# Attention and gated feed-forward on one core: group 0's first keys and queries through identity products, its row maxima on both sides of the array, the turns of heads later

## What is computed

```python
xn = layernorm(x)                                   # x: 1024 tokens x 512, f32
q, k, v = xn@wq+bq, xn@wk+bk, xn@wv+bv              # 32 heads of q, 8 of k and v, 16 values each
q, k = rope(q), rope(k)
s = softmax(q k^T / 4) v                            # each k/v head serves 4 q heads
z = xn@W.T + b
m = sum_e p[e] * (xn@A[e])@B[e]                     # 8 x 16 = rank 128
g = silu(z + min(0.5*|z|/(|m|+1e-6), 1) * m)
out = x + s*g
```

## Time and profile before

| | |
|---|---|
| median of 3 runs | 451.78 us (449.76 to 451.89) |
| the profiled execution | 451.26 us |
| its span | 449.5 us |
| TensorE, matmuls busy | 432.0 us (96%) |
| VectorE busy | 370.5 us (82%) |
| ScalarE busy | 307.3 us (68%) |
| POOL busy | 133.3 us (30%) |
| mean granted TensorE clock | 0.978 of full speed |

### The profile page before, as it was taken

The page is one execution under the profiler, slowest core; times in us unless marked ns, Lnnn a source line. Parts: engine busy times, 40 slices in busy tenths (PEclk is TensorE's granted clock), DMA queues, the critical chain, the costliest instruction groups (busy, mean ns, idle before and its releaser), DMA issues.

```text
span 449.5 us, 8242 instructions
## 1 busy us (share of the span) xinstructions
PE 432.0 (96%) x3141; PEld 190.9 (42%) x3141; DVE 370.5 (82%) x613; ACT 307.3 (68%) x606; POOL 133.3 (30%) x185
## 2 busy tenths in 40 slices
PE   7899899999999999999999999999999999899993
PEld 3466343444344444444444444444434444333330
DVE  5553688888999999999999999999999999723443
ACT  2120011223889898988989988898999889656882
POOL 7562312434203130421313042131304123101544
PEclk9989899999899999999999999999999999999997
DMA  8979954444000020000000000000000000010002
GB/s 261 310 122 125 131 74 70 70 74 71 2 1 3 1 56 1 1 4 1 4 0 3 2 2 4 1 1 1 3 2 3 1 1 4 2 51 35 20 22 65
DMA packets 13624, 18.09 MB, mean 40 GB/s; under 512 B 3168, under 2 KB 7552, under 8 KB 13584
## 3 DMA queue, kind: packets, MB, share of 16 engines
q1 hardware_dynamic: 12064, 16.44, 19.6%
q10 hardware_dynamic: 1520, 1.12, 0.9%
HBM read 6.72 MB, written 2.10 MB: 20 GB/s over the span
## 4 chain that ended last, share of the span: by engine, by line
PE 85%; DMA 4%; SPq 3%; DVE 3%; ACT 2%; issue 2%; POOL 0%; DVEq 0%; ACTq 0%
PE st L1010 31%; PE oT L978 26%; PE sm L918 6%; PE st L858 6%; PE sm L1085 4%; PE oT L1061 3%; DMA kA<-arena 2%; PE sm L987 2%; DMA idb_sb<-in_identb 2%; PE st L1042 2%; PE oT L858 2%; DVE negmax L721 1%; PE st L894 1%; SPq L305 1%; PE sm L1091 1%
## 5 line engine op out<-in xcount | busy, mean ns | idle before, releaser
L729 DVE TENSOR_REDUCE neghalf<-sm 128x1 f32<-128x512 f32 x448 | 270.6, 678 | 4.8 <-PE sm L918 4.8
L638 ACT ACTIVATE arena<-st 128x512 f32<-128x512 f32 x448 | 233.3, 600 | 19.7 <-PE st L1010 15.8
L918 PE MATMUL sm<-kA,qA 48*128 48x512 f32 x512 | 180.9, 446 | 2.0 <-DMA kA<-arena 1.7
L1010 PE MATMUL st<-qA,kA 50*128 50x512 f32 x448 | 156.6, 445 | 1.0 <-ACT arena L638 0.7
L978 PE MATMUL oT<-arena,vg 128*32 128x256 f32 (+3 forms) x1568 | 129.6, 422 | 0.0
L1010 PEld LDWEIGHTS st<-qA,kA 50*128 50x128 f32 x448 | 73.3, 185 | 97.5 <-ACT arena L638 84.4
L918 PEld LDWEIGHTS sm<-kA,qA 48*128 48x128 f32 x512 | 84.3, 185 | 19.6 <-issue 10.7
L486 POOL TENSOR_TENSOR rsum<-junk,consts 128x16 f32<-128x16 f32 x13 | 37.9, 2912 | 86.3 <-ACT junk L610 86.3
L978 PEld LDWEIGHTS oT<-arena,vg 128*32 128x32 f32 x1568 | 33.5, 108 | 46.1 <-issue 38.2
L721 DVE TENSOR_REDUCE negmax<-sm 128x1 f32<-128x1024 f32 x32 | 38.1, 1220 | 13.0 <-PE sm L918 12.7
L556 ACT ACTIVATE arena<-arena 128x512 fp32r<-128x512 f32 x10 | 6.3, 631 | 56.7 <-POOL arena L415 56.7
(11 more groups left out here) (103 smaller groups left out, 325.6 us busy)
## 6 DMA issues: line engine op xcount, KB each, us to landing
qA<-arena SPq DMA_DIRECT2D x48, 128.0 KB, 5.1
x_sb<-in_x SPq DMA_DIRECT2D x8, 256.0 KB, 6.2
kA<-arena SPq DMA_DIRECT2D x12, 128.0 KB, 6.7
wT_sb<-in_wT SPq DMA_DIRECT2D x1, 1024.0 KB, 9.1
out<-x_sb SPq DMA_DIRECT2D x1, 896.0 KB, 4.1
out<-x_sb SPq DMA_DIRECT2D x4, 224.0 KB, 2.0
z_sb<-in_wq SPq DMA_DIRECT2D x1, 768.0 KB, 10.9
qA<-qA SPq DMA_DIRECT2D x2, 192.0 KB, 3.4
```

The source lines that it names most:

```text
L638: act.activation(probs[:, s % PB, h, :], st[:, st_score(0, s, h) % 3, :], ACT.Exp, scale=float(D) ** -0.5).then_inc(st_free, 1)
L729: dve.tensor_reduce(neghalf[:, e // 16, e % 16, j % 2:j % 2 + 1], sm[:, n % 4, :], AX.X, ALU.max, negate=True).then_inc(sm_free, count)
L918: pe.matmul(sm[:, n % 4, :], qA[rows, half, g // 2, h, qt * P:(qt + 1) * P], kA[rows, g // 2, kh * HALF:(kh + 1) * HALF], start=True, stop ...
L1010: pe.matmul(st[:, n % 3, :], kA[rows, g // 2, kt * P:(kt + 1) * P], qA[rows, half, g // 2, h, :], start=True, stop=True).then_inc(st_full, 1)
```

## The change

Four things are done.

1. k's two halves and q's first half get their places for group 0 by TensorE: POOL builds matrices of zeros and identities (`put_col`, in a buffer `early` that shares the place of a later tensor), TensorE multiplies the parts by them (`put_rows`, two matmuls that add up high and low slots in one bank), and ScalarE copies the banks (`put_k`, `put_q`) to `k_first` and to `qA`. The parts of the first three halves lie in a part of `qA` that is written later (`part`), so the ring of buffers starts with the fourth half.
2. An entry's two scores use both sides of the array: `k_first` has keys 0 to 511 in partitions 0 to 47 and keys 512 to 1023 in 64 to 111, and `q_first` holds group 0's queries in 64 to 111. SP fills `q_first` by three DMAs for each half (`first_rows`, semaphore `first_put`), the first of them ahead of k's rows. That place belongs to the last q chunk, whose DMAs therefore wait for 32 and for 64 score matmuls (`sm_full`).
3. v's second half moves behind the first four scores; the entries' counts in `MIXED` are new; `idb_sb` and `bv_sb` get semaphores of their own, so that VectorE's first rope waits for `small_in` at 64; `wv`'s DMA is issued behind the tables and wq.
4. `OUT1_AT` and `OUT0_AT` go from 12 and 44 to 18 and 50.

```diff
-PARTS, PART_BUFS = 2, 3
+PARTS, PART_BUFS, FIRST = 2, 3, 3
...
       + [("k", 0, "dve"), ("xT", 4, "act"), ("xT", 5, "act"), ("q", (0, 0), "dve"), ("xT", 6, "act"), ("xT", 7, "act"),
-         ("k", 1, "dve"), ("q", (0, 1), "dve"), ("v", 0, "dve"), ("v", 1, "dve")])
-MIXED = [("q", (1, 0), 0), ("q", (1, 1), 3), ("u", 0, 4), ("q", (2, 0), 3), ("u", 1, 4), ("q", (2, 1), 3), ("z", 0, 3),
-         ("q", (3, 0), 2), ("z", 1, 3), ("q", (3, 1), 2), ("z", 2, 3), ("z", 3, 2)]
+         ("k", 1, "dve"), ("q", (0, 1), "dve"), ("rows of k", 0, "act")]
+      + [("rows of q", h, "act") for h in range(REP)]
+      + [("v", 0, "dve"), ("rows of k", 1, "act")])
+MIXED = [("q", (1, 0), 2), ("v", 1, 0), ("q", (1, 1), 3), ("u", 0, 3), ("q", (2, 0), 3), ("u", 1, 3), ("q", (2, 1), 3),
+         ("z", 0, 3), ("q", (3, 0), 3), ("z", 1, 3), ("q", (3, 1), 2), ("z", 2, 2), ("z", 3, 2)]
...
-OUT1_AT, OUT0_AT = 12, 44
+OUT1_AT, OUT0_AT = 18, 50
...
         wq_rows = wq_sb.rearrange("p c (k a d h) -> p k a c d h", k=CHUNKS, a=2, h=REP)
+        def part(n, which):
+            if n < FIRST:
+                return qA[:, n // 2, 2, 2 * (n % 2) + which, :]
+            return parts[:, n % PART_BUFS, which, :].bitcast(F32R)
+        with nc.sbuf_tensor("early", [P, TH * E], F32R) as early:
+            k_first = early[0:ROWS + KR, 0:HALF]
+            put_col = early[:, HALF:HALF + 2 * (1 + REP) * P].rearrange("p (k h m) -> p k h m", k=PARTS, m=P)
+        q_first = qA[ROWS:ROWS + KR, :, LAST // 2, :, :]
...
             wq_v = wq.rearrange("(c p) n -> p c n", p=P)
-            sp.dma_start(wv_sb, wv.rearrange("(c p) n -> p c n", p=P)).then_inc(wv_in, 16)
             sp.dma_start(z_sb[:, :, P:E], wq_v[:, :, P:E]).then_inc(wq_in, 16)
+            sp.dma_start(wv_sb, wv.rearrange("(c p) n -> p c n", p=P)).then_inc(wv_in, 16)
             sp.dma_start(p_sb[:, :], p_sc).then_inc(ffn_in, 16)
-            sp.dma_start(idb_sb[:, :], identb).then_inc(small_in, 16)
-            sp.dma_start(bv_sb[:, :], bv.partition_broadcast(P)).then_inc(wv_in, 16)
+            sp.dma_start(idb_sb[:, :], identb).then_inc(idb_in, 16)
+            sp.dma_start(bv_sb[:, :], bv.partition_broadcast(P)).then_inc(bv_in, 16)
...
-                for n in range(len(halves)):
+                for n in (0, *range(2, len(halves))):
...
             sp.wait_ge(ones_set, 1)
+            def first_rows(n, half):
+                for slot in sorted(range(len(Q_SLOTS)), key=lambda k: Q_SLOTS[k]):
+                    sp.wait_ge((part1, part2)[Q_SLOTS[slot]], n + 1)
+                    sp.dma_start(q_first[slot * D:(slot + 1) * D, half, :, :].bitcast(F32),
+                                 part(n, Q_SLOTS[slot])[0:ROWS, :].bitcast(F32)).then_inc(first_put[half], 16)
+            first_rows(halves.index(("q", (0, 0))), 0)
             for n, (kind, i) in enumerate(halves):
+                if (kind, i) == ("q", (0, 0)):
+                    continue
+                if (kind, i) == ("q", (0, 1)):
+                    first_rows(n, 1)
                     maxima_row(0, 0)
+                if (kind, i) == ("q", (2, 0)):
+                    sp.wait_ge(stacked[0], 16 * SLOT_DMAS)
+                    sp.wait_ge(first_put[0], 48)
+                    sp.wait_ge(pj_full, PJ_AT["rows of q", REP - 1] + 1)
+                if (kind, i) == ("q", (2, 1)):
+                    sp.wait_ge(stacked[2], 16 * SLOT_DMAS)
+                    sp.wait_ge(pj_full, PJ_AT["rows of k", 1] + 1)
+                if kind == "q" and i[0] == 3:
+                    sp.wait_ge(sm_full, 32 * (i[1] + 1))
...
                             to = qA[rows, i[1], i[0], :, :]
-                        sp.dma_start(to.bitcast(F32),
-                                     parts[odd * ROWS:(odd + 1) * ROWS, n % PART_BUFS, of_slot[slot], :]
+                        sp.dma_start(to.bitcast(F32), part(n, of_slot[slot])[odd * ROWS:(odd + 1) * ROWS, :].bitcast(F32)
...
                     put_columns(0)
+            pool.memset(put_col.bitcast(F32), 0.0).then_inc(columns_set, 1)
+            pool.wait_ge(columns_set, 1)
+            pool.wait_ge(id_in, 16)
+            came = id_sb[:, :].rearrange("p (a d h) -> p h a d", a=2, h=REP)
+            for slot in range(len(Q_SLOTS)):
+                at = slice(slot * D, (slot + 1) * D)
+                to = put_col[:, Q_SLOTS[slot], 1:, :].rearrange("p h (a r) -> p h a r", a=2)
+                pool.tensor_copy(to[:, :, :, at], came).then_inc(columns_set, 1)
+                for odd in range(2):
+                    to = put_col[:, K_SLOTS[slot], 0, odd * ROWS:(odd + 1) * ROWS]
+                    pool.tensor_copy(to[:, at], came[:, 0, 0, :]).then_inc(columns_set, 1)
...
                 pool.wait_ge(part1, n + 1)
-                pool.tensor_tensor(parts[:, n % PART_BUFS, 1, :].bitcast(F32R), rot[:, n % 2, :],
-                                   parts[:, n % PART_BUFS, 0, :], ALU.subtract).then_inc(part2, 1)
+                pool.tensor_tensor(part(n, 1), rot[:, n % 2, :], part(n, 0).bitcast(F32),
+                                   ALU.subtract).then_inc(part2, 1)
...
                 act.wait_ge(rotated, n + 1)
-                if n >= PART_BUFS:
+                if n == FIRST + PART_BUFS:
+                    act.wait_ge(first_put[1], 48)
+                if n >= FIRST + PART_BUFS:
                     act.wait_ge(stacked[n - PART_BUFS], 16 * SLOT_DMAS)
-                act.activation(parts[:, n % PART_BUFS, 0, :].bitcast(F32R), rot[:, n % 2, :],
-                               ACT.Copy).then_inc(part1, 1)
+                act.activation(part(n, 0), rot[:, n % 2, :], ACT.Copy).then_inc(part1, 1)
+            def put_k(i):
+                e = PJ_AT["rows of k", i]
+                act.wait_ge(pj_full, e + 1)
+                rows = slice(i * ROWS, i * ROWS + KR)
+                act.activation(k_first[rows, :], pj(e)[rows, :], ACT.Copy).then_inc(pj_act, 1)
+            def put_q():
+                for h in range(REP):
+                    e = PJ_AT["rows of q", h]
+                    act.wait_ge(pj_full, e + 1)
+                    act.activation(qA[0:ROWS + KR, 0, 0, h, :], pj(e)[0:ROWS + KR, :], ACT.Copy).then_inc(pj_act, 1)
                 cast(n)
+                if n == 2:
+                    put_k(0)
+                    put_q()
+                if n == 3:
+                    put_k(1)
...
-            dve.wait_ge(small_in, 80)
+            dve.wait_ge(small_in, 64)
                 rope(kind, i)
-            for hh in range(2):
+            def keep_values(hh):
                                 pj(e).rearrange("p (t n) -> p t n", t=TH)).then_inc(pj_dve, 1)
+            keep_values(0)
...
             pe.wait_ge(id_in, 16)
-            for kind, i, _ in PJ[:PJ_AT["v", 0]]:
+            def project_values(hh):
+                n = PJ_AT["v", hh]
+                claim(n)
+                for t in range(TH):
+                    for c in range(NE):
+                        mm = pe.matmul(pj(n)[:, t * P:(t + 1) * P], xT[:, hh, c, t * P:(t + 1) * P], wv_sb[:, c, :],
+                                       start=(c == 0), stop=(c == NE - 1))
+                mm.then_inc(pj_full, 1)
+            def put_rows(kind, i):
+                n = PJ_AT[kind, i]
+                of = halves.index(("k", i) if kind == "rows of k" else ("q", (0, 0)))
+                column = 0 if kind == "rows of k" else 1 + i
+                claim(n)
+                pe.wait_ge(columns_set, 1 + 3 * len(Q_SLOTS))
+                for which, done in ((0, part1), (1, part2)):
+                    pe.wait_ge(done, of + 1)
+                    mm = pe.matmul(pj(n), put_col[:, which, column, :],
+                                   part(of, which), start=(which == 0), stop=(which == 1))
+                mm.then_inc(pj_full, 1)
+            for kind, i, _ in PJ[:PJ_AT["q", (1, 0)]]:
...
                     mm.then_inc(pj_full, 1)
-                else:
+                elif kind == "q":
                     project("q", i, wq_sb, slice(0, P), xT[:, i[1]])
-            pe.wait_ge(wv_in, 32)
-            for hh in range(2):
-                n = PJ_AT["v", hh]
-                claim(n)
-                for t in range(TH):
-                    for c in range(NE):
-                        mm = pe.matmul(pj(n)[:, t * P:(t + 1) * P], xT[:, hh, c, t * P:(t + 1) * P], wv_sb[:, c, :],
-                                       start=(c == 0), stop=(c == NE - 1))
-                mm.then_inc(pj_full, 1)
+                elif kind == "v":
+                    pe.wait_ge(wv_in, 16)
+                    project_values(i)
+                else:
+                    put_rows(kind, i)
...
                 e = next(entries)
-                for n in {0: (0, 1, 2), 16: (3,)}.get(e, ()):
-                    pe.wait_ge(stacked[n], 16 * SLOT_DMAS)
-                for j in (2 * e, 2 * e + 1):
-                    score_rows(0, j, j, 1)
+                if e == 0:
+                    pe.wait_ge(pj_act, emptied(PJ_AT["rows of k", 1])[1])
```

(19 more changed lines are left out.)

10 lines of the change are left out of this document (8 added, 2 removed).

## The result

The changed kernel takes **437.7 us** (median of four runs, 436.6 to 443.2; the 443.2 is an execution with a mean clock of 0.971 where the other three have 0.985 to 0.986). The kernel before took 451.8 beside it; the ratio is 0.969, with a 95% interval of 0.964 to 0.973. The profiled execution took 436.62 us, its span 434.8, against 451.26 and 449.5 before.

A forecast was written before the change was run, and what follows sets the result against it. Row DMAs held the first score, TensorE bounded the mixed stage, VectorE the steady groups. 451.3 - 10.0 (front and stage) - 3.9 (turns) = 437.4; with the runs' median 0.5 higher, 438.0 us; range 434 to 443.5, its own case 435 to 441.

The forecast's parts named there:

- The first score: Front, TensorE's first score for group 0's row maxima: at 37.2 us instead of 46.30.
- The rival of late rows: Front: first score still waits for three DMAs or five copies, at 42 us; kernel 443 us; chance 0.07.
- The identity's wait: VectorE's first rope step: without the wait for the bf16 identity it starts at 17.3 us instead of 20.73.
- The mixed stage: Projections mixed with group 0's row maxima: 62.5 us instead of 64.4, plus 1.0 for extra waits.
- The pairs: Mixed stage, scores on both sides of the array: 32 pairs at 0.25 us less each, -8.0 us.
- Pairs overlap in part: Rival in the mixed stage: a pair costs 0.36 us, half-way back to serial 0.48; kernel 442.2 us; chance 0.09.
- VectorE takes the stage: Rival: VectorE keeps all its idle time before reductions; mixed stage 68.2 us, kernel 442.6 us; chance 0.15.
- The rival of the clock: Mixed stage: TensorE's waits lower its clock, 1.7 us per fall; twelve falls give 458 us; chance 0.03.
- Group 0's first score: End of the mixed stage: the first exponential's score at 100.7 us instead of 110.67, -10.0 us.
- The 13th exponential: ScalarE in group 0: its wait for q's last rows costed at nothing, up to 3 us if landing is slow.
- The turns: Steady groups: 13 of 16 turns of heads move behind a 256-column block, 0.3 us each, -3.9 us.

## Why the prediction was right

**The first score**, 37.2 predicted, 37.67 seen. POOL's nine casts took 2.3 us (2.0 taken), its first sum began at 21.58 (21.5). The pitch from one sum to the next was not 3.25 but 3.4 to 3.7, so k's second half was split at 32.2 (31.3) and v began at 31.75 (31.2). TensorE reached the identity products at 27.2 (28.5) and waited there. The rival of late rows fell: the chain has no DMA, and none is among the waits of the entry scores. The run that waits for the row DMAs shows what late rows would have cost: all of the front's gain and more.

**The identity's wait.** The prediction moved VectorE's rope from 20.73 to 17.3, so that it ends near 19.5, and had POOL free at 21.4 for the first sum. By its own sum POOL's queue was the later of the two, but it did not draw from this that the earlier rope is worth next to nothing, and my expectation of 2 to 4 us for it was wrong. Putting the wait for the identity back costs 0.6 at the first score, moving wq's copies away wins 1.7.

**The mixed stage**, 62.5 + 1.0 predicted, 62.9 from the first score to the last projection before group 0. The pairs are the term that carries it: 0.23 for a further pair, against 0.46 on one side (taken: 0.48), in bursts between 128-row projections too. The Trainium skill, page "TensorE: Matmul & The Clock Gate", section "Measured speedup vs the span model", gives 3.07 of 4 for four row tiles, which I had turned into 0.30 a pair as an estimate. The chain's x4 and x2 (0.66 and 0.43) leave 0.23, so here the measurement decides for full overlap of two. "Pairs overlap in part" falls by the same rows. "VectorE takes the stage" (68.2 us) falls as well: its idle time fell to 7.0, and TensorE waited for it in 14 short waits, of at most 1.0 us, which hold up its weight loads: 10.7 us of them, but only 0.5 us in which no matmul ran. The rival of the clock falls: 1.00 over the stage. It named the stage, and the fall came behind it.

**Group 0's first score**, 100.7 predicted, 101.63 seen, and the step failed by a wait that it had not looked for (timeline of TensorE, kernel after):

```profile
98.56 1.98 PE L934 MATMUL st<-wT_sb,xT_sb 128*128 128x512 f32 x4
101.63 0.47 PE L1122 MATMUL st<-qA,kA 50*128 50x512 f32 x1 [1.08 <-DVE z_sb L846]
```

The last tile of z now lies in the bank that the first score claims, and VectorE must add its bias first. The first exponential is not later for it, since it waits behind ScalarE's squares of that same tile: it came at 102.14, 10.0 earlier. That is the gain which the prediction gave for the score; the score's own is 9.0, and that the exponential makes it 10.0 is luck. Behind the pause the clock falls. The 13th exponential, costed at nothing, waited 0.84 us at 111.88 for its score and not for rows.

**The turns**, -3.9 predicted, 13 x 0.315 = -4.1 seen; of each, about two thirds is distance and one third the smaller block, where the prediction had the block (0.21) in the first place.

**What the prediction left out** is the clock at the starts of group 0 and of the last group. Against the kernel before the first is +1.1 (the 0.8 of the balance, in which one turn's 0.3 is already won), the second -1.6 (the 2.2 less the turns' 0.6). They cancel in part, so 438.0 and 437.7 agree somewhat better than the steps do.

The first of the two is no accident of one execution. All ten profiled executions with the new front, of the changed kernel and of its variants, have a stretch of 4 us at a granted clock of 0.50 to 0.56 within 10 us behind the first exponential. Here is the changed kernel run once more:

```profile
104.00:108.00 4.00, 4.00 (x18) 1.78 (x17) 4.00 (x8) 3.54 (x8) 1.68 (x5) 0.50 0.40 46
```

Of the three with the old front one falls there (the kernel before, to 0.63) and two stay at 1.00. The new front has the pause of 0.88 to 1.09 us ahead of group 0 and another of 0.2 behind its third step; the old front has one of 0.74, in all three. From first exponential to "turn g1" the changed kernel takes 46.4 us and the run of the turns alone, which stays at 1.00, 45.0: the fall costs about 1.4 us. That the wait for the last tile of z brings it is likely by these rows and not shown, since no run takes that wait away.

## What to carry to other kernels

Cost a front part by following every engine's queue, not the one that was last before: here the wait that the profile named was worth 0.6 us after the change and nothing before it, and the engine that had been idle beside it was the next bound. When a wait on a queue of small transfers is last, starting it sooner may not move its end; replace the transfer where the engines have room. Where a fast engine has gaps once per turn, look how far that place lies from the last disturbance: moving the turn away from it gave twice what the shorter block gave.
